# Differential attention: mix transposed before its exponential, pairs of heads in one instruction for short rows, results kept unnormalised

## The reference

```python
energy = jnp.einsum('bqhad,bkhad->bahqk', qd, kd)
causal = jnp.triu(jnp.ones((s, s), dtype=bool), 1)
energy = jnp.where(causal, NEG, energy)
scores = jax.nn.softmax(energy / np.sqrt(D), axis=-1)
lam = (jnp.exp(jnp.sum(lq1 * lk1, -1)) - jnp.exp(jnp.sum(lq2 * lk2, -1)) + LAM_INIT)[None, :, None, None]
diff = scores[:, 0] - lam * scores[:, 1]
diff = jnp.where(causal, NEG, diff)
diff = jax.nn.softmax(diff, axis=-1)
att = jnp.einsum('bhqv,bvhd->bqhd', diff, v)
att = att * jax.lax.rsqrt(jnp.mean(att * att, axis=-1, keepdims=True) + EPS) * rms_w
att = att * (1.0 - LAM_INIT)
return att.reshape(b, s, E) @ Wo
```

## Time and profile before

| | us |
|---|---|
| median of 3 runs (3016.28 to 3024.55) | 3016.36 |
| the profiled execution | 3036.48 |
| span of the profiled execution, first to last instruction | 3034.7 |
| differential attention within it, 1253.1 to 2035.0 | 781.9 |

### The profile page before, as it was taken

One profiled execution on the slowest core, in us unless ns is written; L12 is line 12 of the kernel. 1 busy time (PEld: TensorE's weight loads), 2 busy tenths in 40 slices (PEclk: granted clock), 3 DMA queues, 4 the chain that ended last, 5 costly groups with the idle time before them and its releaser, 6 DMA issues. The chain is left out here.

```text
span 3034.7 us, 68702 instructions
## 1 busy us (share of the span) xinstructions
PE 2472.5 (81%) x25105; PEld 1658.0 (55%) x25192; DVE 2081.4 (69%) x4873; ACT 1836.1 (61%) x3580; POOL 897.9 (30%) x971
## 2 busy tenths in 40 slices
PE   7888868888888698777676677768999686899998
PEld 3433326643333384444344444447888465788988
DVE  5488886677777567799898899974333344666652
ACT  2588964315445443599788898973222333667778
POOL 2233324111111322455455555530000222223223
PEclk9979988969999798899999999988999767899999
DMA  4533302243432113601222022004000656622210
GB/s 158 150 70 69 69 3 100 83 105 57 57 45 26 72 59 109 115 11 20 30 29 28 3 29 29 2 6 167 1 1 1 146 100 99 132 37 32 33 43 8
DMA packets 283034, 177.09 MB, mean 58 GB/s; under 512 B 205649, under 2 KB 242529, under 8 KB 280673
## 3 DMA queue, kind: packets, MB, share of 16 engines
q1 hardware_dynamic: 273552, 164.55, 26.0%
q10 hardware_dynamic: 9168, 8.41, 1.2%
HBM read 113.84 MB, written 54.66 MB: 56 GB/s over the span
## 5 line engine op out<-in xcount | busy, mean ns | idle before, releaser
L1364 ACT ACTIVATE ad_e<-ps,ad_nm 128x1024 f32<-128x1024 f32 (+7 forms) x512 | 383.5, 756 | 81.0 <-DVE ad_nm L1425 78.4
L1425 DVE TENSOR_REDUCE ad_nm<-ps 128x1 f32<-128x1024 f32 (+7 forms) x512 | 369.4, 748 | 36.6 <-PE ps L1293 35.8
L1398 POOL TENSOR_TENSOR ad_e<-ad_e,ad_c 128x128 f32<-128x128 f32 (+7 forms) x256 | 293.3, 1146 | 16.5 <-DVE ad_rz L1438 10.1
L663 ACT ACTIVATE ab_e<-ps 128x512 f32<-128x512 f32 (+3 forms) x384 | 167.1, 491 | 190.6 <-PE ps L578 189.4
L1291 PE MATMUL ps<-fd_k_st,fd_q_st 96*128 96x512 bf16 (+3 forms) x768 | 214.4, 340 | 70.2 <-ACT ad_e L1364 52.0
L388 PE MATMUL ps<-warm,ident_b 128*128 128x512 bf16 x425 | 139.1, 393 | 114.6 <-ACT ad_prT L1349 112.5
L1449 DVE CUSTOM_DVE_ANT_0 ad_t<-ad_e,ad_rz 128x128 f32<-128x128 f32 (+7 forms) x256 | 223.3, 872 | 4.2 <-ACT ad_pr L1372 2.4
L1391 POOL TENSOR_TENSOR ad_e<-ad_e,later_k 128x128 f32<-128x128 f32 x256 | 118.8, 464 | 355.4 <-ACT ad_e L1364 355.4
L1372 ACT ACTIVATE ad_pr<-ad_t,ad_low 128x128 f32<-128x128 f32 (+7 forms) x256 | 200.1, 782 | 0.0
L1306 PE MATMUL ps<-ident,ad_pr 128*128 128x128 f32 x1152 | 175.8, 281 | 24.0 <-ACT ad_pr L1372 24.0
L1910 POOL TENSOR_TENSOR st_it_low<-st_it,st_it_high 128x256 fp32r<-128x256 f32 x128 | 98.5, 782 | 316.9 <-ACT st_it_high L2173 311.5
(11 more groups left out here) (389 smaller groups left out, 7119.3 us busy)
## 6 DMA issues: line engine op xcount, KB each, us to landing
scr_a<-pa_parts SPq DMA_DIRECT2D x24, 512.0 KB, 2.8
fa_q_st<-scr_a SPq DMA_DIRECT2D x24, 512.0 KB, 7.9
...
```

The source lines that it names most:

```text
L663: act.activation(e[:, u % ER, h, lo:QB], m.ps[:, n4(u, h) % 3, lo:QB], ACT.Exp, scale=scale).then_inc(s_read[0], 1)
L1364: act.activation(e[:, u % EB, s, 0:L], src, ACT.Exp, bias=nm[:, u % EB, s:s + 1], accum_out=z[:, u % EB, s:s + 1]).then_inc(exped[s], 1)
L1398: pool.tensor_tensor(e[:, k, 1, 0:L], e[:, k, 1, 0:L], c[:, k:k + 1].to_broadcast([P, L]), ALU.mult).then_inc(mixed, 1)
L1425: dve.tensor_reduce(nm[:, u % EB, s:s + 1], src, AX.X, ALU.max, negate=True).then_inc(maxed[s], 1)
```

## The change

- The mix is transposed before its exponential. `mix` keeps the maximum in `top` (addition with a positive `rz` now). POOL's new `spread_top` multiplies the identity by `top`, and in `turn` PE transposes `t2` into PSUM and adds, with one fp32r matmul per bank (stationary operand -1, moving operand `top_diag`, repeated for each block), minus the row's maximum. ACT's `softmax` then reads PSUM banks 4 and 5 and writes `prT`; `pr`, `copy_turned` and the warming matmuls are gone.
- For short rows, an odd unit and the even one before it (`members(u)`) share one instruction for a maximum, the mask, the scaling of side 1, `spread_top` and the softmax. The exponentials of the two sides stay one per unit. `coefficients` do a pair at a time for all rows, in three small instructions.
- The mask is an affine_select instead of an addition.
- `result` is gone. ACT's `keep_result` copies value sums and row sum as they are, 17 values per head, and `norm_project` applies the row sum through the norm: eps is multiplied by its square. The same function loses an unused second form.
- Lags and orders are new: mix 4 (was 3), turn 6 (was 5), value 7 to 9, copy_out 10, lead 16 (was 14). On DVE the coefficients of long rows and the mix now come ahead of maximum 0.

The diff, without declarations and the parts of `norm_project` that only go:

```diff
+    t2 = ph.sb("t2", [P, 4, T])
+    top = ph.sb("top", [P, EB])
+    minus = ph.sb("minus", [P, P], F32R)
+    top_diag = ph.sb("top_diag", [P, 4, P], F32R)
+    lam_group = ph.sb("lam_group", [P, HG])
...
+    def members(u):
+        return (u,) if place(u)[2] >= 4 else (u - 1, u) if u % 2 else ()
+    def banks(first_bank, units, L):
+        if len(units) == 2:
+            return m.ps[:, first_bank:first_bank + 2, 0:L]
+        return m.ps[:, first_bank:first_bank + 2, :].rearrange("p a n -> p (a n)")[:, 0:L]
...
+                def run(i, u):
+                    for v in members(u):
+                        one(i, v)
                 return run
             def turn(i, u):
                 b, h, t, L = place(u)
-                for x in range(2):
-                    wait(pe, copied[x], i, COPIES[x], copies(u - short_second(u), x))
-                keep_warm(pe, m, 4 + (u % 2 if t < 4 else 0), 2)
-                wait(pe, p_done, i, PER, u + 1)
+                wait(pe, p_done, i, PER, u - short_second(u))
+                wait(pe, lowered, i, PER, u + 1)
                 for kb in range(t + 1):
                     bank = 4 + (u % 2 if t < 4 else kb // 4)
-                    last = pe.transpose(m.ps[:, bank, (kb % 4) * P:(kb % 4 + 1) * P],
-                                        pr[:, u % 2, kb * P:(kb + 1) * P], m.ident[:])
+                    pe.matmul(m.ps[:, bank, (kb % 4) * P:(kb % 4 + 1) * P], t2[:, u % 4, kb * P:(kb + 1) * P], m.ident[:],
+                              is_transpose=True, start=(kb % 4 == 0), stop=True, skip_group_check=True)
+                if u == 0 and (not isinstance(i, int) or i == 0):
+                    pe.wait_ge(minus_set, 2)
+                wait(pe, top_spread, i, PER, u + 1)
+                for cc in range(t // 4 + 1):
+                    bank = 4 + (u % 2 if t < 4 else cc)
+                    blocks = min(4, t + 1 - 4 * cc)
+                    last = pe.matmul(m.ps[:, bank, 0:blocks * P].rearrange("p (k q) -> p k q", q=P), minus[:],
+                                     top_diag[:, u % 4, None, :].to_broadcast([P, blocks, P]),
+                                     start=False, stop=True, skip_group_check=True)
                 last.then_inc(turned, 1)
...
-            pipelined(pe, [(0, score(0)), (5, turn), (0, score(1)), (6, value(0)), (7, value(1)), (8, value(2)),
-                           (10, turn_back)], PER, ITERS, lead=14)
...
-            return run
+            pipelined(pe, [(0, score(0)), (6, turn), (0, score(1)), (7, value(0)), (8, value(1)), (9, value(2)),
+                           (11, turn_back)], PER, ITERS, lead=16)
...
             def softmax(i, u):
+                units = members(u)
+                if not units:
+                    return
                 b, h, t, L = place(u)
-                wait(act, lowered, i, PER, u + 1)
-                wait(act, turned, i, PER, u - 1)
-                act.activation(pr[:, u % 2, 0:L], t2[:, u % 2, 0:L], ACT.Exp, bias=low[:, u % EB:u % EB + 1],
-                               scale=-1.0).then_inc(p_done, 1)
+                wait(act, turned, i, PER, u + 1)
+                wait(act, valued, i, QUADS, u // HG - 1)
+                k = units[0] % (2 * HG)
+                dst = prT[:, k:k + 2, 0:L] if len(units) == 2 else prT[:, k, 0:L]
+                act.activation(dst, banks(4, units, L), ACT.Exp).then_inc(p_done, len(units))
...
+            def keep_result(i, u):
+                b, h, t, L = place(u)
+                if h == HG - 1:
+                    wait(act, returned, i, QUADS, u // HG + 1)
+                    dst = m.y_tok[:, b * BT + t, ds((i + u // PER) * HG, HG), :]
+                    act.copy(dst, m.ps[:, 7, 0:P].rearrange("p (h d) -> p h d", h=HG)[:, :, 0:HD + 1]).then_inc(result_kept, 1)
...
-            pipelined(act, [(0, exps(0)), (4, softmax), (5, copy_turned(act, 1)), (0, exps(1)), (9, copy_out)],
-                      PER, ITERS, lead=14)
+            pipelined(act, [(0, exps(0)), (6, softmax), (0, exps(1)), (10, copy_out), (12, keep_result)],
+                      PER, ITERS, lead=16)
...
             def mask(i, u):
+                units = members(u)
+                if not units:
+                    return
                 b, h, t, L = place(u)
                 wait(pool, exped[0], i, PER, u + 1)
-                tile = e[:, u % EB, 0, t * P:L]
-                pool.tensor_tensor(tile, tile, m.later_k[:], ALU.add).then_inc(masked, 1)
+                pool.sem_inc(maskable, 1)
+                k = units[0] % EB
+                tile = e[:, k:k + len(units), 0, t * P:L]
+                pool.affine_select(out=tile, in_=tile, compare_op=ALU.is_ge, fill=NEG, base=0,
+                                   pattern=[[0, len(units)], [-1, P]], channel_multiplier=1).then_inc(masked, len(units))
...
             def scale_second(i, u):
+                if u % 2 == 0:
+                    return
                 b, h, t, L = place(u)
-                k = u % EB
-                wait(pool, coef, i, 2 * PER, 2 * u + 1)
-                pool.tensor_tensor(e[:, k, 1, 0:L], e[:, k, 1, 0:L], c[:, k:k + 1].to_broadcast([P, L]),
-                                   ALU.mult).then_inc(mixed, 1)
-            pipelined(pool, [(0, mask), (1, scale_second)], PER, ITERS, lead=14)
+                wait(pool, coef, i, PER // 2, u // 2 + 1)
+                k = u % EB - 1
+                if t < 4:
+                    pool.tensor_tensor(e[:, k:k + 2, 1, 0:L], e[:, k:k + 2, 1, 0:L],
+                                       c[:, k:k + 2, None].to_broadcast([P, 2, L]), ALU.mult).then_inc(mixed, 2)
+                    return
+                for x in (k, k + 1):
+                    pool.tensor_tensor(e[:, x, 1, 0:L], e[:, x, 1, 0:L], c[:, x:x + 1].to_broadcast([P, L]),
+                                       ALU.mult).then_inc(mixed, 1)
+            def spread_top(i, u):
+                units = members(u)
+                if not units:
+                    return
+                n, k = len(units), units[0] % 4
+                wait(pool, lowered, i, PER, u + 1)
+                wait(pool, turned, i, PER, u - 3)
+                pool.tensor_tensor(top_diag[:, k:k + n, :], m.ident[:, None, :].to_broadcast([P, n, P]),
+                                   top[:, k:k + n, None].to_broadcast([P, n, P]), ALU.mult).then_inc(top_spread, n)
+            pipelined(pool, [(5, spread_top), (1, mask), (2, scale_second)], PER, ITERS, lead=16)
...
             def maxima(s):
                 def run(i, u):
+                    units = members(u)
+                    if not units:
+                        return
                     b, h, t, L = place(u)
                     wait(dve, scored[s], i, PER, u + 1)
-                    src = m.ps[:, 2 * s + u % 2, 0:L] if t < 4 else \
-                        m.ps[:, 2 * s:2 * s + 2, :].rearrange("p a n -> p (a n)")[:, 0:L]
-                    dve.tensor_reduce(nm[:, u % EB, s:s + 1], src, AX.X, ALU.max, negate=True).then_inc(maxed[s], 1)
+                    n, k = len(units), units[0] % EB
+                    dve.tensor_reduce(nm[:, k:k + n, s], banks(2 * s, units, L), AX.X, ALU.max,
+                                      negate=True).then_inc(maxed[s], n)
                 return run
...
-            def coefficients(i, u):
-                hh = i * HG + (u % HG + HG * (u // PER))
-                k = u % EB
-                wait(dve, exped[0], i, PER, u + 1)
-                wait(dve, exped[1], i, PER, u + 1)
-                dve.reciprocal(rz[:, k, :], z[:, k, :]).then_inc(inv, 1)
-                wait(dve, inv, i, PER, u + 2)
-                dve.scalar_tensor_tensor(c[:, k:k + 1], rz[:, k, 1:2], nlam[:, ds(hh, 1)], z[:, k, 0:1],
-                                         ALU.mult, ALU.mult).then_inc(coef, 1)
-                dve.tensor_scalar(rz[:, k, 0:1], rz[:, k, 0:1], -1.0, None, ALU.mult).then_inc(coef, 1)
+            def coefficients(long):
+                def run(i, u):
+                    if u % 2 == 0 or (place(u)[2] >= 4) != long:
+                        return
+                    k, h = u % EB - 1, u % HG - 1
+                    if u % PER == 1:
+                        dve.tensor_copy(lam_group[:], nlam[:, ds((i + u // PER) * HG, HG)]).then_inc(lam_chosen, 1)
+                    wait(dve, exped[0], i, PER, u + 1)
+                    wait(dve, exped[1], i, PER, u + 1)
+                    dve.reciprocal(rz[:, k:k + 2, :], z[:, k:k + 2, :]).then_inc(inv, 1)
+                    wait(dve, lam_chosen, i, 1, u // PER + 1)
+                    dve.tensor_tensor(c[:, k:k + 2], z[:, k:k + 2, 0], lam_group[:, h:h + 2], ALU.mult).then_inc(weighted_z, 1)
+                    wait(dve, weighted_z, i, PER // 2, u // 2 + 1)
+                    wait(dve, inv, i, PER // 2, u // 2 + 2)
+                    dve.tensor_tensor(c[:, k:k + 2], c[:, k:k + 2], rz[:, k:k + 2, 1], ALU.mult).then_inc(coef, 1)
+                return run
...
             def mix(i, u):
```

(18 more changed lines are left out.)

132 lines of the change are left out of this document (33 added, 99 removed).

## The result

| | before, us | after, us |
|---|---|---|
| median (range, runs) | 3019.36 (3016.28 to 3024.55, 4) | 3213.14 (3198.75 to 3228.96, 4) |
| profiled execution's span | 3034.7 | 3210.5 |
| differential attention within the span | 781.9 | 958.6 |

The ratio is 1.063, 95% interval 1.060 to 1.066: the change costs 194 us, where 3014 was forecast and 3046 was the upper bound. In the two profiled executions, whose spans lie 175.8 us apart, differential attention takes 176.7 us more, 22 us for each of the eight halves; what lies ahead of it is 12 us longer and the scan behind it 14 us shorter, in code that the change doesn't touch. The 194 us of the medians are more than that because the profiled execution of before, at 3036.5 us, lay 17 us above its median.

A forecast was written before the change was run, and what follows sets the result against it. Long rows were taken as bound by the shared port of DVE and POOL, short rows by waits for scaling. One half: 17.3 + 20.0 + 56.3 = 93.6 against 94.0 us; eight halves -3 us, forecast 3014 us, range 2965 to 3046.

The forecast's parts named there:

- DVE and ACT as the bounds of before: Long rows: both engines busy 97 to 100% of the time, so whatever leaves them comes back as time.
- The start of the odd mix: Long rows, DVE: the odd slot's mix starts just ahead of POOL's scaling and takes 1.15 us at t = 7.
- Rival B: Long rows: POOL's first scaling takes the port before the odd mix, which waits 1.7 us; +28 us, 3042; chance 0.20.
- Loop 1: Long rows: score 1 waits for the previous unit's exponential 1; a floor of 8.2 us for two units at t = 7.
- Loop 2: Long rows: mix and POOL's scaling exclude each other; 0.13 + 2M + 2S + 2X = 8.6 us per two slots at t = 7.
- Short rows: Per half: DVE waits for the pair's scaling, 20.0 us against 19.7 (t = 2, 3); 17.3 against 19.1 (t = 0, 1).
- rival C: PE: without warming matmuls the TensorE clock falls; +6 us per half, +50 us, 3064; chance 0.06.
- the pace at t = 7: Sign in the changed kernel's profile that the likeliest case holds: 4.35 us per unit at t = 7.
- mixes that are all long: Sign of Rival B in the profile: all mixes of 1024 columns over 1.9 us, not only the even ones.

The follow-up runs named there:

- e11: Kernel before, with only the results kept unnormalised (a DVE copy) and the new norm: 3011.91 us, ratio 0.997.
- e3: Changed kernel with the mix ahead of the long rows' coefficients on DVE: 3100.70 us, ratio 1.026.
- e4: Changed kernel with PE's turn behind both scores instead of between them: 3182.41 us, ratio 1.054.
- e6: Changed kernel with both the edits of e3 and e4: 3097.42 us, ratio 1.026.
- e14: e10 with the scalings of two long rows back to back again: 3014.82 us, ratio 0.999.
- e9: e3 with short rows one unit per instruction again, no pairs: 3056.91 us, ratio 1.011.
- e16: e10 with short rows in pairs again, but their scores, maxima and exponentials one unit at a time: 3052.38 us, ratio 1.009.
- e10: e7 with eight rows of exponentials in the ring instead of four: 2975.36 us, ratio 0.985.
- e2: Kernel before, with only the warming matmuls of turn taken out: 3052.08 us, ratio 1.010.
- e1: Changed kernel with the two warming matmuls put back ahead of each turn: 3241.05 us, ratio 1.071.
- e12: Changed kernel with eight rows of exponentials in the ring instead of four: 3203.82 us, ratio 1.060.
- e7: Changed kernel with DVE's order of before, long scalings one per slot and no pairs in short rows: 3116.78 us, ratio 1.032.

## Why the prediction was wrong

**DVE and ACT as the bounds of before**: right for t = 5 to 7. At t = 4 ACT was busy 83% (10.17 of 12.20 us), not 97 to 100%, and DVE alone was full. e11 got its 10 us from DVE alone.

**The start of the odd mix** is the step that failed most. The second loop assumed that "the mix of that odd slot starts just ahead of" POOL's scaling. It doesn't: 0.24 us idle behind the last coefficient, and POOL is there 0.15 us earlier. Rival B had the mechanism and its condition (a start later than 0.1 us after the coefficients), with chance 0.20, but priced it at 28 us; e3 shows 112. The price was too small because I added the 1.7 us to a sum of DVE's own work, 9.1 us for two slots, and not to the ring through ACT and PE: the 11.4 us of the timeline are that sum and 2.3 us in which DVE waits for scores.

**Loop 1** was built on "score 1 of the next unit waits for exponential 1 of this one", and on nothing of PE's own order. I had counted the turn as busy time of PE, not as a step of a chain; but it stands between score 0 and score 1 in PE's queue, and took 2.25 us there. With it and the race the ring takes 11.4 us, where the forecast's loop took 8.2. The turn's share is 31 us (e4), which the race's removal also gives (e6).

**Loop 2**, the shared port, was right in mechanism and in size, but was not what bound the changed kernel: the loop keeps the even mix waiting until both scalings are over, but that mix ran free at 1478.01, in 1.14 us. Where its assumptions hold, in e14, t = 4 to 7 take 10.9, 12.6, 14.4 and 16.4 us, or 5.5, 6.3, 7.2 and 8.2 per two units against 5.7, 6.7, 7.6 and 8.6 forecast.

**Short rows** were forecast 0.3 us per half slower for t = 2 and 3 and 1.8 faster for t = 0 and 1. Pairs cost 5.7 us per half (e9). I charged the scaling and `spread_top` ahead of the mix, and missed that a pair takes both score banks. No row of before could show it, but the code does: `banks` gives a pair both. By e16 that is about a third of what pairs cost in e10's order; the rest isn't explained.

**The clock** (rival C, chance 0.06, 50 us): it fell from 0.96 to 0.77 over the stage, although PE is busy for 71% of t = 7 (18.07 of 25.31 us), the very share that I had named against it. Its price was 29 us in the kernel before (e2), and in the changed one raising it by warming matmuls made the time longer (e1); what the lower level costs inside the ring wasn't separated. In e10 it is at 1.00 for t = 5 to 7 without them.

**The new lag against the ring** was not in the prediction at all. It costs nothing as the change stands (e12), but it closes the way back: the order that avoids the race runs into it (e7).

In sum, from after (3213): mix first -112, no pairs -44, and 3057 is left, 34 over before. That is near the 29 us which the missing warming matmuls cost before, but no run puts them back into e9, so the match is not shown to be the cause. The parts of the change that remain in e10 are worth 45 us together with the wider ring.

The signs I had named told it in part: the pace at t = 7 was not 4.35 us per unit but 5.7. For B I had named mixes that are all long, and they weren't: the odd ones were and the even ones weren't, since the shut-out mix takes the port from the second scaling and the next one finds it free.
